# Spreading the output projections of attention over the tiles, and x with the first heads' weights as one transfer a chunk

## The reference

```python
q = (x @ Wq.T + bq).reshape(B, T, 16, 128).transpose(0, 2, 1, 3)
k = x @ Wk.T + bk                       # one head of 128 for all 16
v = x @ Wv.T + bv
mask = pos[None, :] < pos[:, None]
scores = where(mask, einsum('bhtd,bsd->bhts', q, k) / sqrt(128), -1e30)
attn = softmax(scores) * row_valid
out = einsum('bhts,bsd->bhtd', attn, v).transpose(0, 2, 1, 3).reshape(B, T, 2048)
x = layernorm(x + out @ Wo.T + bo)
hidden = fwht(silu(x @ W1.T) * (x @ W3.T))
x = layernorm(x + hidden @ W2.T)
```

## Time and profile before

| what | value |
|---|---|
| median of 3 runs | 2031.18 us (2029.46 to 2032.61) |
| the profiled execution's own time | 2031.74 us |
| its span, slowest core (core 7) | 2030.2 us; the cores 2023.7 to 2030.2 us |
| mean granted TensorE clock, core 7 | 0.996 |
| PE busy | 1951.9 us, 96% |
| ACT, DVE, POOL busy | 517.6, 365.2, 225.4 us |
| DMA | 227.81 MB, mean 112 GB/s |

### The profile page before, as it was taken

The page is one execution under the profiler, slowest core; times in us unless marked ns, Lnnn a source line. Parts: engine busy times, 40 slices in busy tenths (PEclk is TensorE's granted clock), DMA queues, the critical chain, the costliest instruction groups (busy, mean ns, idle before and its releaser), DMA issues.

```text
span 2030.2 us, 32675 instructions; the slowest of 8 cores (2023.7 to 2030.2 us)
## 1 busy us (share of the span) xinstructions
PE 1951.9 (96%) x11200; PEld 966.0 (48%) x11200; DVE 365.2 (18%) x670; ACT 517.6 (25%) x967; POOL 225.4 (11%) x250
## 2 busy tenths in 40 slices
PE   8999788889999999999999999999999999999997
PEld 3555455555564444444444444444444444444443
DVE  1113443332223110000001100000012310042111
ACT  0002467778881111111111111111112200031001
POOL 1002711100103000000000000000004200020000
PEclk9999999999999999999999999999999999999999
DMA  8567200000002333323232332333336945584554
GB/s 273 179 205 249 74 1 2 2 2 2 2 2 72 100 91 91 97 86 101 81 104 89 93 92 90 102 106 98 89 100 199 309 148 155 154 246 156 152 154 141
DMA packets 103494, 227.81 MB, mean 112 GB/s; under 512 B 10336, under 2 KB 43392, under 8 KB 100912
## 3 DMA queue, kind: packets, MB, share of 16 engines
q1 hardware_dynamic: 76128, 126.90, 20.0%
q0 software_dynamic: 27216, 98.82, 16.5%
HBM read 200.52 MB, written 25.17 MB: 111 GB/s over the span
## 4 chain that ended last, share of the span: by engine, by line
PE 90%; DVE 4%; issue 2%; ACT 2%; DMA 1%; SPq 0%; DVEq 0%; ACTq 0%; POOL 0%; POOLq 0%
PE PS L306 90%; ACT GA L851 1%; DMA GA<-WQS 1%; DVE GA L650 1%; DVE GA L684 1%; DVE GA L668 1%; DMA GA<-HIDD 0%; DVE PS L712 0%; DVE RS L646 0%; DVE RS L644 0%; SPq L991 0%; DVE LNS L755 0%; DVE GA L753 0%; DVE GA L679 0%; DVE LNS L670 0%
## 5 line engine op out<-in xcount | busy, mean ns | idle before, releaser
L306 PE MATMUL PS<-GA 128*128 128x512 bf16 (+2 forms) x10688 | 1923.3, 337 | 43.4 <-ACT GA L851 16.4
L306 PEld LDWEIGHTS PS<-GA 128*128 128x128 bf16 x10688 | 928.0, 98 | 989.7 <-issue 106.5
L851 ACT ACTIVATE GA<-PS 128x512 bf16<-128x512 f32 (+1 forms) x576 | 303.1, 561 | 136.5 <-DVE PS L712 73.4
L875 ACT ACTIVATE GA<-PS 128x512 f32<-128x512 f32 x128 | 76.4, 597 | 765.7 <-PE PS L306 765.7
L737 DVE TENSOR_TENSOR GA<-GA,PS 128x512 bf16<-128x512 f32 x128 | 88.0, 688 | 816.5 <-PE PS L306 816.5
L885 ACT CAST GA<-PS 128x512 bf16<-128x512 f32 x64 | 37.0, 585 | 255.4 <-PE PS L306 255.4
L959 POOL DMA_DIRECT2D GA<-W1S x62 | 32.8, 530 | 610.8 <-PE PS L306 610.8
L306 PE MATMUL PS<-GA,CB 128*128 128x512 bf16 x256 | 96.0, 379 | 1.2 <-DMA GA<-HIDD 0.6
L943 POOL TENSOR_SCALAR GA<-GA,LNS 128x2048 f32<-128x2048 f32 x8 | 57.9, 7235 | 261.8 <-DVE GA L679 261.8
L869 ACT ACTIVATE GA<-PS 128x512 bf16<-128x512 f32 x128 | 75.7, 592 | 0.6 <-PE PS L306 0.6
L975 POOL DMA_DIRECT2D GA<-HIDD x64 | 45.3, 711 | 245.1 <-PE PS L306 224.2
(11 more groups left out here) (41 smaller groups left out, 211.4 us busy)
## 6 DMA issues: line engine op xcount, KB each, us to landing
GA<-W2S SPq DMA_DIRECT2D x256, 256.0 KB, 2.8
GA<-W1S POOLq DMA_DIRECT2D x64, 512.0 KB, 4.2
GA<-W3S POOLq DMA_DIRECT2D x64, 512.0 KB, 3.9
GA<-XBT SPq DMA_DIRECT2D x8, 2048.0 KB, 12.9
HIDD<-GA SPq DMA_DIRECT2D x128, 128.0 KB, 3.5
GA<-HIDD POOLq DMA_DIRECT2D x64, 256.0 KB, 10.9
GA<-WOS SPq DMA_DIRECT2D x4, 2048.0 KB, 17.5
GA<-XOWN SPq DMA_DIRECT2D x8, 1024.0 KB, 12.5
```

What stands on the lines that cost most here:

```text
L306: return e.matmul(out, lhsT, rhs, start=start, stop=stop, skip_group_check=True)
L851: e.activation(heads(p_tile(k, g, it))[:, :, cs], heads(pb[score_bank(nn)])[:, :, cs], AF.Exp, scale=SC).then_inc(sE, 1)
L875: e.activation(silu[n % 2], pb[g_bank(n)][:], AF.Silu).then_inc(sSil, 1)
```

## The change

In attention: (1) the turned attention result is written over the q that it came from (`attnT4 = qT4`), so a row tile's result stays until it is used; `turned` no longer waits for the projection two row tiles before. (2) The places of the projections count over all 576 steps: row tile k's begins at `o_from(k)` = 23 + 79k, its 64 products are spread over 54 positions with one position left out between quarters (for row tile 6: 48 products over 54 positions and the same gaps, its last quarter behind the last step), `rstd` is at +61, `norm` at +64, and the four turns at +67, +69, +71, +73. (3) The turn of a unit's attention result is at step 5 of the next unit instead of 3, from row tile 2 on (`turn_at`). (4) The bias of the output projection is loaded once, whole, and added a row tile at a time, in order; a row tile's first output add waits for its own bias add alone.

In the front: (5) x and the first four heads' weights come as one array `XW`, 16 chunks of 1536 columns, one transfer and one semaphore a chunk, in the order of use. (6) The other heads have six weight buffers instead of eight, and GpSimd issues them when chunk 12 is there, from head 7 on each behind the end of head h-4. (7) SP issues the first block of Wo behind the 16th head instead of the 12th, and the second behind the first row tile.

```diff
-    XTOWN = nc.dram_tensor("XTOWN", [128, DC * 1024], BF16, kind="ExternalInput")
-    WQS = nc.dram_tensor("WQS", [128, DC * 512], BF16, kind="ExternalInput")
+    XW = nc.dram_tensor("XW", [128, DC * 1536], BF16, kind="ExternalInput")
...
-        boh = vf(O_BO, 1024)
-        attnT = [vb(O_AT + i * 4096, 2048) for i in range(2)]
+        bo = vf(O_BO, 2048)
+        attnT4 = qT4
...
-        def o_at(k, i):
-            if k < J - 1:
-                return 6 + i * (steps(k) - 18) // 64
-            return 6 + i * (steps(k) - 8) // 48 if i < 48 else steps(k)
+        def o_from(k):
+            return 23 + 79 * k
+        def o_at(k, i):
+            if k == J - 2 and i >= 48:
+                return NT
+            return o_from(k) + (72 if k == J - 2 else 54) * i // 64 + i // 16
         def rstd_at(k):
-            return steps(k) - 9
+            return o_from(k) + 61
         def norm_at(k):
-            return steps(k) - 7
+            return o_from(k) + 64
         def xt_at(k, c4):
-            return steps(k) - 5 + c4
+            return o_from(k) + 67 + 2 * c4
+        def turn_at(u):
+            return 3 if u < 2 * NG else 5
...
+            def q_mm(h, c, w):
+                for th in range(2):
+                    m = mm(pb[q_bank(h) + th][:], w, xw3[:, c, th * 512:th * 512 + 512],
+                           c == 0, c == DC - 1)
+                if c == DC - 1:
+                    m.then_inc(tQ, 1)
...
-            for i, (c0, c1) in enumerate(pieces):
-                e.wait_ge(dXT[i], 16)
-                e.wait_ge(dWQ0[i], 16)
-                for c in range(c0, c1):
-                    ...
+            for c in range(DC):
+                e.wait_ge(dXW[c], 16)
+                for h in range(4):
+                    q_mm(h, c, xw3[:, c, 1024 + h * 128:1024 + h * 128 + 128])
...
-                m = mm(pb[bank][:], attnT[k % 2][:, h * 128:h * 128 + 128],
+                m = mm(pb[bank][:], attnT4[:, k, h, :],
                        woB[oc][:, h * 512:h * 512 + 512], h == 0, h == HN - 1)
...
+            def beside(nn):
...
+                for k in range(J - 1):
+                    for i in range(64):
+                        if o_at(k, i) == nn:
+                            if i == 0 and k == 0:
+                                e.wait_ge(vV, 8)
+                            elif i == 0:
+                                e.wait_ge(vXT, 4 * k)
+                            elif i % 16 == 0:
+                                e.wait_ge(vO, 4 * k + i // 16)
+                            o_mm(k, i, 6)
+                    for c4 in range(4):
+                        if k < J - 2 and xt_at(k, c4) == nn:
+                            ...
+                            x1_turn(k, c4, 6)
...
-                        if it == 3 and u > 0:
+                        if it == turn_at(u) and u > 0:
                             turn(u - 1)
-                        beside(k, 4 * (k + 1) * g + it)
+                        beside(nn)
...
             def turned(u):
                 e.wait_ge(tAT, u + 1)
-                if k >= 2:
-                    e.wait_ge(tO, 4 * (k - 1))
-                e.tensor_copy(attnT[k % 2][:, g * 512:g * 512 + 512],
-                              pb[av_bank(u)][:]).then_inc(vAT, 1)
+                e.tensor_copy(attnT4[:, k, 4 * g:4 * g + 4, :],
+                              heads(pb[av_bank(u)])).then_inc(vAT, 1)
...
                 if oc == 0:
-                    e.wait_ge(pBO, 4 if k < 2 else 16)
+                    e.wait_ge(pBO, k + 1)
...
-            e.wait_ge(dXT[4], 16)
+            e.wait_ge(dXW[12], 16)
             for h in range(4, 16):
-                if h >= 8:
+                if h >= 7:
                     e.wait_ge(tQ, h - 3)
-                e.dma_start(wqh[(h - 4) % 8], WQH[h - 4]).then_inc(dWQH[(h - 4) % 8], 16)
+                e.dma_start(wqh[(h - 4) % 6], WQH[h - 4]).then_inc(dWQH[(h - 4) % 6], 16)
...
+            e.dma_start(bo, BOR[:]).then_inc(dBO, 16)
+            e.wait_ge(dBO, 16)
+            for k in range(J):
+                r = R[:, k * 2048:k * 2048 + 2048]
+                e.wait_ge(dR[k], 16)
+                e.tensor_add(r, r, bo).then_inc(pBO, 1)
...
-            for i, (c0, c1) in enumerate(pieces):
-                e.dma_start(xTown[:, c0 * 1024:c1 * 1024],
-                            XTOWN[:, c0 * 1024:c1 * 1024]).then_inc(dXT[i], 16)
-                e.dma_start(wq0[:, c0 * 512:c1 * 512], WQS[:, c0 * 512:c1 * 512]).then_inc(dWQ0[i], 16)
+            for c in range(DC):
+                e.dma_start(xw3[:, c, :], XW[:, c * 1536:c * 1536 + 1536]).then_inc(dXW[c], 16)
...
-            e.wait_ge(tQ, 12)
+            e.wait_ge(tQ, 16)
             e.dma_start(woB[0], WOS[0]).then_inc(dWO[0], 16)
-            e.wait_ge(tQ, 16)
-            e.dma_start(woB[1], WOS[1]).then_inc(dWO[1], 16)
             e.wait_ge(tV, 6)
             r_load(0)
+            e.dma_start(woB[1], WOS[1]).then_inc(dWO[1], 16)
```

More of the change, by code:

```diff
@@ L163, in build_program @@
         O_AN = 191488
[L164 to L165 removed]
+        O_BO = 197632
         O_XTM = 205824
@@ L194, in build_program @@
         xtb = [vb(O_XTB + i * 16384, 8192) for i in (1, 2, 0)]
[L195 to L200, removed]
+        wqh = [vb(O_WQ + i * 4096, 2048) for i in range(6)]
+        xw3 = vb(O_XW, DC * 1536).rearrange("p (c x) -> p c x", c=DC)
         w1b = [vb(O_C + i * 4096, 2048) for i in range(2)]
@@ new lines, in beside @@
+            def beside(nn):
+                for blk in (6, 7):
+                    for c in range(16):
+                        if kv_at(blk, 0, c) == nn:
+                            if c == 0:
+                                e.wait_ge(dXTB[blk % 3], 48)
+                                if blk == 6:
+                                    e.wait_ge(sK, 6)
+                                else:
+                                    e.wait_ge(vV, 7)
+                            k_mm(blk, c)
+                    for i in range(64):
+                        if kv_at(blk, 1, i) == nn:
+                            if i == 0:
+                                e.wait_ge(sK, blk + 1)
+                            v_mm(blk, i)
+                for k in range(J - 1):
+                    for i in range(64):
+                        if o_at(k, i) == nn:
[8 more added lines that the diff above has]
+                        if k < J - 2 and xt_at(k, c4) == nn:
+                            if c4 == 0:
+                                e.wait_ge(vO, 4 * k + 4)
+                            else:
+                                e.wait_ge(vXT, 4 * k + c4)
+                            x1_turn(k, c4, 6)
@@ L684, in x1_turned, with beside @@
                 e.tensor_copy(x1T4[:, k, c4 * 4:c4 * 4 + 4, :], heads(pb[bank])).then_inc(vXT, 1)
-            def beside(k, t):
-                if k == 0:
-                    for blk in (6, 7):
-                        if kv_at(blk, 1, 63) == t:
-                            v_out(blk)
-                    return
-                for oc in range(4):
-                    if o_at(k, 16 * oc + 15) == t:
-                        o_out(k - 1, oc, 6)
-                if k < J - 1 and norm_at(k) == t:
-                    norm(k - 1)
-                for c4 in range(4):
-                    if k < J - 1 and xt_at(k, c4) == t:
-                        x1_turned(k - 1, c4, 6)
+            def beside(nn):
+                for blk in (6, 7):
+                    if kv_at(blk, 1, 63) == nn:
+                        v_out(blk)
+                for k in range(J - 1):
+                    for oc in range(4):
+                        if o_at(k, 16 * oc + 15) == nn:
+                            o_out(k, oc, 6)
+                    if k < J - 2 and norm_at(k) == nn:
+                        norm(k)
+                    for c4 in range(4):
+                        if k < J - 2 and xt_at(k, c4) == nn:
+                            x1_turned(k, c4, 6)
             e.wait_ge(dMask, 16)
```

106 lines of the change are left out of this document (19 added, 87 removed).

## The result

| | before | after |
|---|---|---|
| median of four runs | 2031.38 us | 1996.28 us |
| ratio, with its 95% interval | | 0.9827 (0.981 to 0.9844) |
| span of the slowest core | 2030.2 us | 1994.5 us |
| first q add on DVE, median of the cores | 39.0 us | 33.7 us |
| attention: from the first mask add to GpSimd's first W1 issue, median | 442.6 us | 411.7 us |

The change takes 35.1 us off, 1.7%. The front gives 5.3 us, attention 30.9, the rest nothing. In some executions of any of these kernels the cores of one die run at a lower granted clock and take some per cent longer; all ratios and times given here are of the others.

The account below looks back on a forecast made before the run. Attention was taken as bound by hand-offs, mostly PE waiting for DVE, with no engine full. Attention's -31.4 us, less 4 given back, and the front's -3.5 sum to -30.9 from 2031.74: 2000 us, 8-in-10 range 1990 to 2017.

Parts of the forecast that it names:

- Output adds: Attention: PE's 12.1 us of waits for DVE's output adds fall to 1.5: -10.6 us (bounds -12.1 and -5).
- Division: Attention: the later turn of the result cuts PE's 10.5 us of waits for the division: -7.8 us (bounds -10 and -4).
- Exponentials: Attention: PE's 16.4 us of waits, from masks behind DVE's work and ACT's pace, change by -2.4 us (bounds -9 and +6).
- rival (a): Attention: masks stay late behind output adds and statistics on DVE, half of the 27.4 us comes back: 2014 us; chance 0.20.
- Clock at the end: End of attention: no late output add, so the slow granted clock (0.64 for 4 us) goes: -1.4 us (bounds 0 and -1.4).
- The 4 us given back: Attention: allowance for the next-latest engine showing once waits are removed; turns the sum of -31.4 into -27.4 us.
- The front: First four heads: smaller transfers in order of use let PE end earlier: -3.5 us (bounds -7.7 and 0).
- What costs nothing: Dropped tO wait, whole bias adds (about 4.7 us each, same total), later Wo and head 7 weight loads: no time change.
- (b): Front: small transfers are paid in turn, +6 us instead of -3.5, so 2010 us; chance 0.08.
- (c): Whole gain exceeds the sum: the 4 us stay out, L851 (exponentials' waits) falls by 9, front gives 6: 1987 us; chance 0.10.
- (d): Attention: places don't matter, each DVE wait removed becomes an equal ACT wait; only the front stays, 2028 us; chance 0.03.
- (e): Attention: granted clock drops to 1.2 GHz in plain steps, +48 us over 164 positions, so 2048 us; chance 0.02.

Follow-up runs that it names:

- the front alone: The kernel before with the changed kernel's front (chunks, six weight buffers, first block of Wo later), attention as before: 2033.7 us against 2033.4, ratio 1.0006.
- run 16: Not a follow-up run: "in the last plain run 16 exponentials start" means 16 exponentials in a run of plain steps of the changed kernel.
- the distances alone: Changed kernel with projections as dense as before, keeping the step between quarters, x1 turns two steps apart, result's turn at step 5: 2008.3 us, ratio 0.988 to kernel before.
- the even load alone: Changed kernel with projections spread over 57 positions, no step between quarters, x1 turns in successive steps, result's turn at step 3: 2020.5 us, ratio 0.9938 to kernel before.

## Why the prediction was right, step by step

The forecast was 2000 us with a range of 1990 to 2017, the time 1996.3. The mechanism is the one named: attention's time went in hand-offs with DVE, and three edits of places took them out. Of the 4.2 us by which the gain of 35.1 exceeds the 30.9 forecast, 4 are the allowance that wasn't needed. By terms, on core 7 where nothing else is said:

- *Output adds*: 1.5 us left was forecast, 3.8 measured: -8.3, not -10.6. The step between quarters is enough only where DVE is free: with the turn back at step 3, 0.8 us are left, so my edit of the turn made some 3 us of these waits.
- *Division*: 1.1 us left instead of 2.7, -9.4 and not -7.8. I gave the first eight units a quarter of the waits; in the rows of before one of them waited, since products lay beside the others. The whole edit is worth 7.2 us of time; that this is near the 7.8 is chance, since waits for output adds and PE's busy time changed with it.
- *x1 copies*: 0.2 us left instead of 1.5, -9.8.
- *Exponentials*: 15.0 us, inside the 14 to 18 forecast. The split was wrong, and the number partly luck. I put most of it down to ACT's pace in plain steps (16.8 us by the step prices). Of the listed waits 7.9 us are five masks behind an output add and its statistics, which rival (a) had named, and 5.8 of the 15.0 went when adds, norms and copies left the diagonal steps. The price of ACT's pace was too high as well: in the last plain run 16 exponentials start in 7.97 us (561.54 to 569.51), 0.50 us each and not 0.569, so a plain step loses 0.07 us, not 0.139. And what that run of steps loses stands in PE's busy time, not in the list of waits.
- *Clock at the end*: 1.00 where it was 0.64, and the 20 matmuls behind the last steps took 3.84 us instead of 5.37: -1.5. The mark between the stages lies 1 us into these matmuls, so it belongs to the last stage, and there it doesn't show: PE's waits for HIDD grew (0.6 to 2.1 us on core 7), and the medians of that stage are equal.
- *The 4 us given back*: little of the kind. The sum without them is -31.4, or -30.0 without the clock at the end; attention lost 30.9 us on the median core, 29.1 on core 7. The close fit is partly luck: by the windows of core 5, PE's idle time fell by 26.1 us (52.6 to 26.5), and 5.2 us are a shorter busy time for the same 3693 matmuls (390.3 to 385.1), which has no term in the sum. The plain positions that fell from 208 to 164 may be a part of it; no run separates the parts.
- *The front*: -3.5 forecast, -5.3 measured on the median core, -6.7 on core 7. The sum for core 7 ended the four heads at 37.2 us, and they ended at 34.8 (13.95 + 20.88). Two sizes were off: chunk 1, which I took as late as piece 1 before (9.44 us), was there when PE had done chunk 0 at 8.4, and the 1.7 us of slow clock did not come: behind chunk 0 no wait was over 0.34 us, and the matmuls kept their 0.2175 us each. Head 4's weight was issued at 23.88 us, with no wait for it.
- *What costs nothing*: here the prediction was right by luck. I gave the bias adds no part in the gain. The run of the front alone shows that with the halves as before the front gives 0 and not 3.5, DVE waiting 5.3 us for GpSimd's add; and with the whole load but the norm at its old place the norm meets the adds, and attention is 3.9 us longer. The slack that I worked out (15 us; 27 measured) is for the first output add in the new order, and I didn't ask about the norm or about the old order.

Of the rivals, (b) failed: 16 transfers landed as fast as 12. (c) came true in two of its three parts: the 4 us stayed out and the front gave more, but L851 did not fall by 9. (d) and (e) failed: no new wait took the place of the old, and the granted clock in attention is 0.99 on cores 3 and 7, where attention took 413.3 us against the median's 411.7, and 1.00 on the others; what made that dip on some cores was not tried. The Trainium skill's rule on transfers of 1 MiB and more ("DMA: Bandwidth & Descriptors", Rules for kernel authors) does not decide here: transfers of 384 KB in order of use beat pieces of up to 1.5 MB by 4.8 us, at no more bytes per second (241 GB/s on core 7 over the first 20 us, against 258).

## What to carry to other kernels

When three engines pass one bank around, count the time from one user's end to the next one's start and put that many steps of other work between; here the distances alone gave two thirds of attention's gain, the even load alone less than a quarter, and both together the whole. Place long vector instructions away from steps in which the same engine stands in the chain of another (a mask in front of an exponential). And when a stage ends earlier, look at every chain that doesn't: a bias load, and then a norm of DVE that met adds of GpSimd, took the front's whole gain until the order behind it was changed. A list of waits is not all: an engine that counts as busy can still be paced by another, so compare its busy time for the same work too.

## What the runs showed of the hardware

- DVE's norm of 2048 elements (float32 in, bf16 out) takes 1.34 us alone and 2.4 to 5.2 us when it begins during one of GpSimd's adds of 4.5 us each; it ended 1.08 to 1.10 us behind that add's end on all eight cores. DVE's output add, with one input in PSUM, kept its 0.69 us during the same adds.
- The order of issue alone doesn't settle when a small transfer is there: with two transfers a chunk, the second chunk was in time on some cores and 2.9 us late on another, in one execution.
- Behind a wait of PE of 3.33 us inside a busy stage the granted clock was 0.50 for 3.7 us, and four turns took 0.58 us instead of 0.38.
- ACT's exponentials of 128x512 out of PSUM have records of 0.60 us each, and start 0.50 us apart when nothing holds them.
